# Second attention of pairs 1 to 3 in a two-layer tower: the rows of its heads come by DMA through DRAM instead of from spreading products

## The reference

```python
xn = (x - mu) / jnp.sqrt(var + 1e-05) * ln_g + ln_b
q = (xn @ wq).reshape(B, S, H, hd)          # H = 32, hd = 8
k = (xn @ wk).reshape(B, S, H, hd)
v = (xn @ wv).reshape(B, S, H, hd)
att = jnp.einsum('bqhd,bkhd->bhqk', q, k) / np.float32(np.sqrt(hd))
p = jax.nn.softmax(att, axis=-1)
o = jnp.einsum('bhqk,bkhd->bqhd', p, v).reshape(B, S, D) @ wo + x
```

## Time and profile before

| | us |
|---|---|
| median of 3 runs (1400.92 to 1402.03) | 1401.38 |
| the profiled execution, own time | 1397.64 |
| its span, first to last instruction | 1395.8 |
| PE busy in the span | 1067.5 (76%) |
| VectorE busy | 734.2 (53%) |
| ScalarE busy | 492.1 (35%) |
| all spreading products of pairs 0 to 3 | 256 on PE, with 64 evictions |
| mean granted TensorE clock | 0.85 of full speed |

### The profile page before, as it was taken

The page is one execution under the profiler, slowest core; times in us unless marked ns, Lnnn a source line. Parts: engine busy times, 40 slices in busy tenths (PEclk is TensorE's granted clock), DMA queues, the critical chain, the costliest instruction groups (busy, mean ns, idle before and its releaser), DMA issues. The chain is left out here.

```text
span 1395.8 us, 23281 instructions
## 1 busy us (share of the span) xinstructions
PE 1067.5 (76%) x8552; PEld 784.0 (56%) x8552; DVE 734.2 (53%) x1910; ACT 492.1 (35%) x988; POOL 153.5 (11%) x210
## 2 busy tenths in 40 slices
PE   1239978897989896997878988875503999999980
PEld 1225745444665465663446635734502999999980
DVE  7972445664536756548666463445140444444446
ACT  2111423454554443544535652520000333333322
POOL 4950000000000000000000000000044111111110
PEclk7558987888999899999989996985555999999995
DMA  9221020000121000120000300200982111111105
GB/s 236 60 72 31 1 76 15 1 16 1 31 84 31 16 2 1 46 69 31 1 1 17 105 25 1 76 0 0 327 321 78 31 40 39 39 39 32 39 32 180
DMA packets 62445, 78.29 MB, mean 56 GB/s; under 512 B 14640, under 2 KB 52288, under 8 KB 62208
## 3 DMA queue, kind: packets, MB, share of 16 engines
q1 hardware_dynamic: 57088, 62.11, 14.1%
q0 software_dynamic: 4672, 14.57, 3.3%
q10 hardware_dynamic: 576, 0.13, 0.0%
HBM read 55.94 MB, written 20.85 MB: 55 GB/s over the span
## 5 line engine op out<-in xcount | busy, mean ns | idle before, releaser
L1499 DVE TENSOR_REDUCE mx<-scores_ps 128x4 f32<-128x1024 f32 (+1 forms) x160 | 186.9, 1168 | 129.6 <-PE scores_ps L1007 78.9
L1348 ACT ACTIVATE pt<-turned_ps 128x1024 f32<-128x1024 f32 (+1 forms) x160 | 157.9, 987 | 148.2 <-PE turned_ps L1029 104.3
L1956 PEld LDWEIGHTS x_ps<-x_xtT,x_w1s 128*128 128x128 f32 x1248 | 147.2, 194 | 3.5 <-ACT x_xtT L1991 1.6
L1956 PE MATMUL x_ps<-x_xtT,x_w1s 128*128 128x128 f32 x1248 | 147.7, 277 | 1.0 <-ACT x_xtT L1991 1.0
L1968 PE MATMUL x_ps<-x_w,x_hT 128*128 x624 | 141.0, 379 | 0.0
L1968 PEld LDWEIGHTS x_ps<-x_w,x_hT 128*128 128x128 f32 x624 | 115.6, 190 | 14.1
L2103 DVE COPY x_w1s<-x_w 128x2048 f32 x39 | 55.3, 1421 | 81.2 <-PE x_ps L1956 64.7
L1019 PE MATMUL turned_ps<-q,k 32*128 32x256 f32 x512 | 71.5, 353 | 29.5 <-DVE mx L1499 21.6
L957 POOL COPY vpad<-v 128x64 f32<-128x64 f32 x64 | 13.9, 248 | 720.6 <-PE ps L1068 590.5
L1019 PEld LDWEIGHTS turned_ps<-q,k 32*128 32x128 f32 x512 | 44.2, 203 | 85.0 <-issue 45.9
L1991 ACT COPY x_xtT<-x_ps 128x256 f32<-128x256 f32 x39 | 14.5, 372 | 218.2 <-PE x_ps L1938 218.2
(11 more groups left out here) (419 smaller groups left out, 1984.9 us busy)
## 6 DMA issues: line engine op xcount, KB each, us to landing
wexp<-in_L_ffn_w SPq DMA_DIRECT2D x16, 1024.0 KB, 5.2
x_w<-in_L_ffn_W SPq DMA_DIRECT2D x16, 1024.0 KB, 13.2
x_slots<-s_zero POOLq DMA_DIRECT2D x1, 5070.0 KB, 33.6
x_xt<-x_slots SPq DMA_DIRECT2D x39, 130.0 KB, 2.1
ha<-h SPq DMA_DIRECT2D x16, 256.0 KB, 3.0
x_pair<-y_rows SPq DMA_DIRECT2D x4, 1024.0 KB, 9.5
x<-hb SPq DMA_DIRECT2D x8, 256.0 KB, 2.5
x_acc<-x SPq DMA_DIRECT2D x4, 512.0 KB, 6.1
```

The costliest lines, as they stand in the source:

```text
L1348: sc.activation(pt[v.index // 2 % (PT_RING // 2)][:, :, 0:wide], turned_ps[:, :, 0:wide], ACT.Exp)\
L1499: v.tensor_reduce(mx[:, u.group % 2, 0:blocks, u.n:u.n + 2].rearrange("p b n -> p n b"), scores_ps[:, :, 0:blocks * (P if u.causal else T) ...
L1956: last = mm(ps[2 * (i % 2) + f // KH][:, f % KH * P:(f % KH + 1) * P], w1s[:, i % 2, c, f * P:(f + 1) * P], xtT[:, i % 2, c, :], start=c = ...
```

## The change

For pairs 1 to 3, stage Y2 becomes `Y2d`, which ends after the six projections, and the stages `Y2s` of these pairs are gone; pair 0 is left as it was. In their place, SP stores the four `nat` tiles of a pair (128 partitions x 1024 values, 512 KB each) to a new DRAM tensor `heads` as soon as `n3` is evicted. It then waits for these stores and for the half of `q1` and `k1` to be free, and loads it with 32 DMAs, each of 8 rows x 8 tiles x 256 values (64 KB, in runs of 1 KB): for each of `q_hi`, `q_lo`, `k_hi`, `k_lo` two groups of rows (`PARTS`) times four. PE waits for all 32 before the first score of the half. The evictions of the next pair's `n0` to `n3`, and those of stage Y1b on side a, which reuse the memory of `nat`, wait for the stores.

```diff
+        "Y2d": [ ... as "Y2" up to "w0", "w1", without SPREAD ... ]
-    ORDER = {"a": (("Y3", 0), ("Y3", 1), ("Y2", 0), ("Y2s", 0), ("Y3", 2), ("Y2", 1), ("Y2s", 1), ("Y3", 3), ("Y2", 2),
-                   ("Y2s", 2), ("Y2", 3), ("Y2s", 3), ("Y1b", 2)),
+    ORDER = {"a": (("Y3", 0), ("Y3", 1), ("Y2", 0), ("Y2s", 0), ("Y3", 2), ("Y2d", 1), ("Y3", 3), ("Y2d", 2), ("Y2d", 3),
+                   ("Y1b", 2)),
...
+            after("Y2d", p, 12, "X1", p, 0)
...
+        def store_natural(p):
+            acted(sp, "n3", p)
+            added(sp, "n3", p)
+            for w, which in enumerate("qk"):
+                for h, part in enumerate(("_hi", "_lo")):
+                    sp.dma_start(heads[p, w, h].rearrange("t f n -> f t n"),
+                                 nat[which + part][:, :, :].bitcast(fp32)).then_inc(sg("nat_out"), 16)
...
+        def load_heads(p, bb):
+
+            reached[p, bb] += 1
+            if reached[p, bb] < 2:
+                return
+            sp.wait_ge(sg("nat_out"), 64 * p)
+            sp.wait_ge(sg("st_full"), half_free(p, bb))
+            for w, (dst, which) in enumerate(((q1, "q"), (k1, "k"))):
+                for h, part in enumerate(("_hi", "_lo")):
+                    rows = heads[p, w, h].rearrange("t (a r d) n -> r d (t a) n", a=4, r=4)
+                    for quarter in cn.PARTS[which + part]:
+                        for r in range(4):
+                            at = 32 * r + 8 * quarter
+                            sp.dma_start(dst[at:at + 8, bb, :, :].bitcast(fp32), rows[r, :, :, bb * T:(bb + 1) * T])\
+                                .then_inc(sg(f"heads_in{bb}"), 16)
...
+                        if s == plan.start["X1", p - 1] + 16 * (bb + 1) + ST_LAG:
+                            load_heads(p, bb)
...
+                if stage == "Y2d":
+                    yield from pause(6)
+                    store_natural(p)
+                    for bb in range(2):
+                        load_heads(p, bb)
...
-                if not u.causal and u.head == 0:
+                if not u.causal and u.head == 0 and u.pair == 0:
                     acted(pe, f"ks{u.bb}2", u.pair)
                     added(pe, f"ks{u.bb}3", u.pair)
+                elif not u.causal and u.head == 0:
+                    pe.wait_ge(sg(f"heads_in{u.bb}"), 16 * 32 * u.pair)
...
+            if p >= 2:
+                act.wait_ge(sg("nat_out"), 64 * (p - 1))
...
+            if p == 0:
+                yield from spreading(p, 0)
+    heads = nc.dram_tensor("heads", (PAIRS, 2, 2, 2, P, TOK), fp32).ap()
```

More of the change, by code:

```diff
@@ L567 @@
               [(a, b, c, d, e.format(0)) for a, b, c, d, e in SPREAD],
+        "Y2d": [(.95, .7, .6, True, "p0_t0 p0_t1"), (1.75, 1.7, 0, True, "p0_0"), (1.75, 1.7, 0, False, "p0_1"),
+                (0, 3, 0, True, ""), (0, 2.8, 0, True, ""), (0, 1.8, 0, True, ""),
+                (.95, .8, .8, True, "xn_t0 xn_t1")] +
+               [(1.75, .7, .6, n == 0, f"n{n}") for n in range(4)] +
+               [(1.75, 0, .6, False, "w0"), (1.75, 0, .6, False, "w1")],
         "Y2s": [(a, b, c, d, e.format(1)) for a, b, c, d, e in SPREAD],
@@ L620, in side, with second @@
         return next((side for side in "ab" if (stage, p) in self.ORDER[side]), "x")
+    def second(self, p):
+        return "Y2d" if p else "Y2"
     def needs(self, work):
@@ L632, in needs @@
             after("Y2", p, 16, "X1", p, 0)
+            after("Y2d", p, 12, "X1", p, 0)
             after("Y2s", p, 3, "X1", p, 16)
-            after("X0", p, 7 + AV_LAG + 2, "Y2", p, 0)
+            after("X0", p, 7 + AV_LAG + 2, self.second(p), p, 0)
             after("X1", p, 31 + AV_LAG + 2, "Y1a", p, 0)
-            after("Y2", p - 1, 0, "X0", p, 1 + AV_LAG + 2)
+            after(self.second(p - 1), p - 1, 0, "X0", p, 1 + AV_LAG + 2)
             after("Y1a", p - 1, 0, "X1", p, 1 + AV_LAG + 2)
@@ L640, in needs @@
                 after("X0", p - 1 - (p == 2), 7 + AV_LAG, "Y3", p, 5)
-            after("Y1b", p - 3, 22, "Y2", p, 6)
-            after("X1", p - 1, 15 + AV_LAG, "Y2", p, 11)
+            after("Y1b", p - 3, 22, self.second(p), p, 6)
+            after("X1", p - 1, 15 + AV_LAG, self.second(p), p, 11)
             after("X1", p - 1, 31 + ST_LAG, "Y2s", p, 0)
@@ L755, in done, with main_loop @@
         return self.freed[self.at[name, p]]
[L758 removed]
+def main_loop(nc, ctx, whole, io, h0, x3, heads, ident, weights, consts):
     plan = Plan()
@@ L896, in a_stream @@
                     continue
-                if stage == "Y2":
+                if stage in ("Y2", "Y2d"):
                     yield from pause(6)
                     next_ha(stage, p, "xn_t1")
+                if stage == "Y2d":
+                    yield from pause(6)
+                    store_natural(p)
+                    for bb in range(2):
+                        load_heads(p, bb)
+                    yield
+                    continue
                 yield from pause(len(plan.STAGES[stage]) - (6 if stage == "Y2" else 0))
@@ L1178, in y2 @@
                 yield
-            evicted("n3", p)
-            yield from spreading(p, 0)
+            if p == 0:
+                evicted("n3", p)
+                yield from spreading(p, 0)
         def spreading(p, bb):
@@ L1307, in a_stream @@
             for stage, p in plan.ORDER["a"]:
-                yield from {"Y3": y3, "Y2": y2, "Y2s": y2s, "Y1b": y1b}[stage](p)
+                yield from {"Y3": y3, "Y2": y2, "Y2d": y2, "Y2s": y2s, "Y1b": y1b}[stage](p)
         def b_stream():
@@ L1394, in y2 @@
                 yield
-            yield from spreading(p, 0)
+            if p == 0:
+                yield from spreading(p, 0)
         def spreading(p, bb):
-            if half_free(p, bb):
-                act.wait_ge(sg("st_full"), half_free(p, bb))
             for j in (0, 2):
@@ L1603, in y2 @@
             yield
-            dve.wait_ge(sg("ha_in"), ha_loaded("Y2", p))
+            dve.wait_ge(sg("ha_in"), ha_loaded(plan.second(p), p))
             for n in range(2):
@@ L1632, in y2 @@
             yield from pause(2)
-            yield from spreading(p, 0)
+            if p == 0:
+                yield from spreading(p, 0)
         def spreading(p, bb):
-            if half_free(p, bb):
-                dve.wait_ge(sg("st_full"), half_free(p, bb))
             for j in (1, 3):
```

12 lines of the change are left out of this document (10 added, 2 removed).

## The result

The changed kernel takes **1394.4 us** (median; 1385.1 to 1400.0) beside 1402.7 of the kernel before on the same chips: a ratio of **0.9927**, 95% interval 0.9907 to 0.9946. The ratio leaves out three of the 20 executions of before, 1431.7 to 1433.1 us, that ran in a slower state of the chip, and compares means, 1393.3 and 1403.5. The forecast was 1392. By the medians the kernel is faster by 8.3 us where 9.4 were forecast. But several terms of the sum were off, and they cancelled.

The account below looks back on a forecast made before the run. PE was taken as the scarce engine, with DMA engines idle. 1397.6 - 25 gained on PE + 15 waiting at pair 3 + 1 slower clock = 1388.6; the median, 3.7 higher, 1392 us; 80% range 1375 to 1430.

Parts of the forecast that it names:

- The products: PE: 192 spreading products in 24 slots go, 16 x 0.55 + 8 x 1.0 = 16.8 us gained.
- The waits: PE idles 20.8 us before the 24 spreading slots; half, 10 us, given back, less about 2 for attention steps standing alone.
- The stores: Four stores of 512 KB after n3's last eviction: 8 us to the last landing (6 to 10).
- The loads: 32 loads of 64 KB a half: 0.8 us each plus 2 to land, 28 us; chance of 0.6 to 1.0: 0.30.
- A pace other than 0.8: Sign that the forecast is wrong: a load goes at another pace than 0.8 us.
- The time there was: Pair 3, between n3 and the first score: 21 us, against 36 for stores and loads.
- one wait, at pair 3 alone: PE waits for the loads once, at pair 3's first score, about 15 us; pairs 1, 2 and second halves hidden.
- After the wait: PE starts at the slower clock after the 15 us wait at pair 3: 1 us lost.
- The pace of the issue: Rival: loads go at SP's issue pace, 0.48 us each; pair 3 waits 4 us, 1380 us in all; chance 0.28.
- The few partitions: Rival: few partitions set 1.2 us a load; PE waits at pairs 2 and 3, 1427 us in all; chance 0.28.
- turning point: Load pace, about 1.0 us, from which the few-partitions case decides, where waits and gain are equal.
- The gain is not there: Rival: the slots' waits pass to what comes next; 15 us gained, waiting at pair 3 takes them: 1402 us; chance 0.10.

Follow-up runs that it names:

- e7: Changed kernel with its 32 loads a half carrying only 4 of 8 tiles (32 KB), the other tiles keeping old values; 1372.0 us, one run.
- e1: Changed kernel with the heads' rows reordered so that the 8 partitions of each load lie 4 apart; 1384.7 us, ratio 0.984.
- e5: Changed kernel, but pair 3 spreads its heads on PE as before; pairs 1 and 2 keep the stores and loads; 1396.3 us, ratio 0.994.
- e9: e5 without the stores and loads of pairs 1 and 2 and the waits for them, on old values; 1393.3 us, ratio 0.992.
- e2: Changed kernel with 32 loads of 64 KB a half, each to 32 partitions 4 apart, two tiles each; 1382.4 us, ratio 0.983.
- e4: Changed kernel without the stores and loads of pairs 1 to 3 and all waits for them, on old values; 1367.3 us, ratio 0.971.
- e10: Kernel with 8 loads of 256 KB a half (32 partitions 4 apart), but pair 3's second half spreads on PE; 1367.4 us, ratio 0.972.

## Why the prediction was right, and where it was not

**The products**: forecast 16.8 us, of them 8 for the eight slots at the slower clock. The clock line gives **11.9** for 192 products, which is 24 x 0.5 at the faster clock, and puts what the slower clock adds into a term of its own. The size of a slot, 0.55, was about right.

**The waits**: forecast 10 of the 20.8 given back, less 2 for bare steps, 8 in all. Without DMA PE idles **10.2** us less than before. Right in size. In the changed kernel the idling outside the wait for heads fell by more, 14.8.

**What was missing** is the clock as a term of the gain: with fewer waits PE works 21.5 us less at the slower clock, **9.6** us, of which the forecast had 8 x 0.45 = 3.6 in its slots. So the gain without DMA is 31.4 by the loops, not 25, inside the range of 15 to 33; by the times of all runs it is 41 (33 to 49), above its upper end. The terms here account for the 31.4 alone.

**The stores**: 6.8 us, forecast 8 (6 to 10). Right.

**The loads**: the step that was mis-sized. 0.8 us each and 28 for the half was forecast, 33.3 came: **1.0 us**, the very end of the range 0.6 to 1.0. A pace other than 0.8 was one of the forecast's own signs of being wrong. I had placed it between issue and landing of the nearest stores, as if it were a price of one DMA. The runs show that at pair 3 it is a price of bytes into neighbours (e7, e1), and that the issue alone would have been 0.34 with its gap, not 0.48.

**The time there was**: 18.2 us, forecast 21. The 27.4 us of before from which I started ran at a mean clock of 0.88, these 18.2 at 1.00. By an estimate with the clock line that alone is about 2 us.

So the wait at pair 3 was 21.9, not 15: 1.2 less for the stores, 5.3 more for the loads, 2.8 for the stretch. That it would be one wait, at pair 3 alone, with pairs 1 and 2, the second halves and the expert weights all hidden, held in every point: the table of waits of the whole loop has no other row for a DMA of these. At pair 2 this was close. From `n3` (503.17) to the first score (542.49) there were 39.3 us, forecast 38, and the 6.7 of the stores and 33.3 of loads at the pace of pair 3 would have been 40. e5 and e9 confirm that the DMAs of pairs 1 and 2 cost nothing.

**After the wait**: forecast 1 us of slower clock. Beside the kernel without DMA, PE did 20.9 us more work at the slower clock, **9.4 us** by the line. None of it lies in the loop's last 92 us, where both are busy for 60.3. By the stretches of 1 us about 14 of the 20.9 lie within 60 us behind the wait, some 6 us of time; most of the rest is a stretch at 839 to 860, and whether the wait has to do with that is not shown. In size the term takes back the whole gain by the clock.

The loop by measured terms, after beside before: -11.9 for the products, -0.3 for the clock (together -12.1 in PE's busy time), -14.8 of other idling (152.5 less 21.9, beside 145.4), +21.9 of waiting: -5.0. The forecast had -16.8 + 1, -8 and +15: -8.8. More waiting stands against more waits given back. That the median came within 2.4 us of the forecast is thus partly luck.

**The rivals.** The pace of the issue does set in once the rows lie apart (e1, e2), but at 0.7 us a load, not 0.48. The few partitions are the right mechanism at pair 3, at 1.0 and not 1.2 us: 1.2 was the middle of two rows here, and the Trainium skill's estimate as well. My turning point "from 1.0 us on" was placed with a gain of 25; the gain without DMA is at least 31.4, so it lies higher. "The gain is not there" is refuted by e4.

## What to carry to other kernels

Where a step goes from an engine to the DMA queues and its landing is waited for, look at what it lands on: choose the layout so that one DMA writes partitions that lie apart, and make it large. Here rows apart turned 33 us for 2 MB into 25, and large loads on top of that into about 9, and 8 us of gain into 36; large loads to neighbours were not tried. Price a DMA with three limits, issue, destination and engines, and take the worst. Where PE waits in a few places, forecast the clock with the work: kernels with the same products differed by 14 us of PE's busy time, 0.45 us for each microsecond of work at the slower level, and one arrangement with four small slots cost more than 20 by the clock.

## What the runs showed of the hardware that I had not expected

- SP's issue time depends on the shape of the destination and not on the bytes: 306 ns for 8 neighbouring partitions (64 KB), 301 for 32 KB, 426 for 16 neighbours, 655 for 8 partitions 4 apart, 600 and 614 for 32 partitions 4 apart at 64 and at 256 KB.
- 1 KB runs out of DRAM into 32 partitions move at 300 GB/s, 54 ns a run as in the earlier trace rows; into 8 neighbours a run takes 123 ns at pair 3, but 47 ns late in the loads of pair 2, for a reason that no run shows.
- PE can be busy for 31 of 34 us and stay at the slower clock (e5, e9), while after a similar fall it is back in 10 (e10).
